# Attention on one core: value products of two key blocks together, at the later step

## What is computed

```python
# per batch b: n = 512 tokens, 8 heads, query/key width 64, value width 16
x = layernorm(x)
q, k = split(x @ W_qk); v = x @ W_v
dots = einsum('bhid,bhjd->bhij', q, k) * SCALE
attn = softmax(dots + bias[None], axis=-1)
out  = einsum('bhij,bhjd->bhid', attn, v)
out  = out.reshape(b, n, 128) @ W_out + b_out
```

## Time and profile before

| | us |
|---|---|
| median of 3 runs (lowest, highest) | 1367.31 (1366.61, 1368.74) |
| the profiled execution | 1359.86 |
| its span, first to last instruction | 1358.1 |
| TensorE busy in the span | 1087.7 (80%) |
| VectorE busy | 957.2 (70%) |
| ScalarE busy | 898.7 (66%) |
| GpSimd busy | 513.2 (38%) |

### The profile page before, as it was taken

The page is one execution under the profiler, slowest core; times in us unless marked ns, Lnnn a source line. Parts: engine busy times, 40 slices in busy tenths (PEclk is TensorE's granted clock), DMA queues, the critical chain, the costliest instruction groups (busy, mean ns, idle before and its releaser), DMA issues. The chain is left out here.

```text
span 1358.1 us, 26011 instructions
## 1 busy us (share of the span) xinstructions
PE 1087.7 (80%) x7230; PEld 732.7 (54%) x7230; DVE 957.2 (70%) x2037; ACT 898.7 (66%) x1865; POOL 513.2 (38%) x318
## 2 busy tenths in 40 slices
PE   1776488878788787863895899999999999992697
PEld 1333366666666675651894345454454445541696
DVE  5899577778788788854664467685776768673465
ACT  1787698989889798941673466665766566660564
POOL 0467377677767767861443000101101010111244
PEclk9888699899899899977998799999999999995899
DMA  3000132223254235321332100000000000000321
GB/s 83 2 3 2 32 87 86 74 84 93 78 173 133 91 116 156 90 67 51 95 94 63 47 1 1 17 1 17 13 3 16 1 16 0 16 17 33 97 88 49
DMA packets 50616, 74.26 MB, mean 55 GB/s; under 512 B 7351, under 2 KB 28604, under 8 KB 50528
## 3 DMA queue, kind: packets, MB, share of 16 engines
q1 hardware_dynamic: 41504, 51.09, 13.2%
q0 software_dynamic: 5568, 12.66, 2.6%
q10 hardware_dynamic: 3456, 9.46, 2.3%
HBM read 57.86 MB, written 16.24 MB: 55 GB/s over the span
## 5 line engine op out<-in xcount | busy, mean ns | idle before, releaser
L951 DVE TENSOR_TENSOR_SCAN h<-d_a,p_dbu 128x1024 f32<-128x1024 f32 x128 | 291.0, 2282 | 79.3 <-ACT d_a L738 55.4
L685 POOL TENSOR_TENSOR h<-h,c_rep 128x1024 f32<-128x1024 f32 x128 | 301.5, 2366 | 113.9 <-DMA c_rep<-c_rows 71.1
L1833 ACT ACTIVATE at_probs<-at_scores,at_min 128x512 f32<-128x512 f32 x256 | 183.7, 722 | 136.0 <-DVE at_min L1943 87.0
L1195 POOL DMA_INDIRECT expert_rows<-r_row,r_dest x64 | 62.9, 982 | 503.7 <-DVEq L1121 488.2
L1943 DVE CUSTOM_DVE_ANT_0 at_scores<-at_p_scores,arena 128x512 f32<-128x512 f32 x256 | 174.4, 684 | 89.8 <-PE at_p_scores L1709 50.2
L828 PE MATMUL p_dbu<-ident,b_du_T 128*128 128x128 f32 x1024 | 189.6, 306 | 55.4 <-ACT b_du_T L731 52.9
L731 ACT ACTIVATE b_du_T<-arena,b_T 128x256 f32<-128x256 f32 (+1 forms) x512 | 216.9, 496 | 0.3 <-ACT arena L712 0.2
L828 PEld LDWEIGHTS p_dbu<-ident,b_du_T 128*128 128x128 f32 x1024 | 117.2, 150 | 119.9 <-issue 66.8
L738 ACT ACTIVATE d_a<-arena,a_exp 128x511 f32<-128x511 f32 (+1 forms) x256 | 169.3, 710 | 0.7 <-DVE h L951 0.6
L1716 PE MATMUL at_p_probs_T<-ident,at_probs 128*128 128x128 f32 x1024 | 158.9, 283 | 5.3 <-ACT at_probs L1833 4.6
L1716 PEld LDWEIGHTS at_p_probs_T<-ident,at_probs 128*128 128x128 f32 x1024 | 112.7, 142 | 91.2 <-issue 68.0
(11 more groups left out here) (211 smaller groups left out, 1484.1 us busy)
## 6 DMA issues: line engine op xcount, KB each, us to landing
c_rep<-c_rows SPq DMA_DIRECT2D x128, 256.0 KB, 3.3
f_row<-expert_rows SPq DMA_DIRECT2D x78, 129.0 KB
arena<-in_w_all ACTq DMA_DIRECT2D x8, 578.0 KB, 4.0
arena<-bias_by_distance ACTq DMA_DIRECT2D x8, 448.0 KB, 3.8
x_tok<-in_x SPq DMA_DIRECT2D x4, 512.0 KB, 5.4
x_tok<-x_between SPq DMA_DIRECT2D x8, 256.0 KB, 2.8
expert_rows<-f_pad SPq DMA_DIRECT2D x10, 129.0 KB, 3.1
expert_rows<-f_pad ACTq DMA_DIRECT2D x8, 129.0 KB, 3.1
```

The source lines that it names most:

```text
L685: nc.gpsimd.tensor_tensor(h[:, s % HS, :, :], h[:, s % HS, :, :], cc, ALU.mult).then_inc(prod_done, 1)
L951: nc.vector.tensor_tensor_scan(h[:, s % HS, :, :].rearrange("p c t -> p (c t)"), da[:, s % 2, :, :].rearrange("p c t -> p (c t)"), p_dbu[: ...
L1833: nc.scalar.activation(pr[:, s % 2, :], sc[:, s % 2, :], ACT.Exp, scale=-1.0, bias=mn[:, s % 2:s % 2 + 1]).then_inc(probs_ready, 1)
```

## The change

The key blocks 0 and 1 of a group, which were issued at two steps, are issued together at the second of them, and the key blocks 2 and 3 likewise. Six steps of a batch (10, 14, 18, 22, 26, 30) lose their 8 records, six (12, 16, 20, 23, 28, 31) have 16 in place of 8. Nothing else is changed.

```diff
--- before.py
+++ after.py
@@ -1719,8 +1719,8 @@
 
 
             VALUES_AT = {}
-            for v, at in enumerate(((10, 12, 14, 16), (18, 20, 22, 23), (26, 28, 30, 31))):
-                VALUES_AT.update({s: (v, j, j + 1) for j, s in enumerate(at)})
+            for v, at in enumerate(((12, 16), (20, 23), (28, 31))):
+                VALUES_AT.update({s: (v, 2 * j, 2 * j + 2) for j, s in enumerate(at)})
 
             def values(b, par, v, first, end):
```

## The result

The changed kernel takes 1373.45 us (median of 11 runs, 1370.32 to 1378.54), the kernel before 1366.61 us (median of 11 runs beside it, 1362.50 to 1370.01). The ratio is 1.0047, 95% interval 1.0032 to 1.0062: **slower by 0.47%, 6.4 us (4.4 to 8.5)**. The forecast was slower, by 3.4 us; the time lies in the range, the size was about half of what came. Measured again twice, the ratio was 1.0042 (1.0026 to 1.0058) and 1.0029 (1.0012 to 1.0047): 5.7 and 4.0 us. The mean of the three is 5.4 us.

What follows compares the result with a forecast made beforehand. Attention looked TensorE-bound, but waits between engines decide what a moved group brings. Six middle batches +2.28, jumps -0.26, first batch +0.18, last +1.18 gave +3.4 us on the median 1367.3: 1370.7 us, range 1366.0 to 1374.0.

Steps and rivals of the forecast that it cites:

- Steps 10 to 15: Middle batches: removals at steps 10 and 14 bring 0, the enlarged step 12 arrives in full at the logits; sum +0.43.
- the 0.43 of step 12: Step 12's group grows from 0.57 to 1.00 us, delaying its turn and, through a tight chain, the router's logits.
- Steps 16 to 0: Rest of a middle batch: additions of 0.43 against removals of up to 0.57, sum -0.05 us.
- step 18: Turn 19 must wait for exponential 19, so of the 0.57 removed only 0.19 us is gained.
- First and last batch: First batch, without router, +0.18 us; last batch, without projections or next scores as cover, +1.18 us.
- The jumps: Two loop jumps between batches: step 30's whole 0.57 comes through in place of 0.44, 2 x -0.13 = -0.26 us.
- Rival (c): The clock stays up at the two jumps: 3.4 - 1.2 = +2.2 us, 1369.5; chance 0.10.

Runs made afterwards that it cites:

- Filling the waits: Identity transposes added in TensorE's waits of steps 11 and 15: to the changed kernel (ratios to before 1.0018, 1.0003), to only the first group merged (1.0044, 1.0037).
- unfilled kernels: The changed kernel (ratios to before 1.0042, 1.0029) and the kernel before with only the first value group merged (1.0067), both without added transposes.

## Why the prediction was right in its sign and too small

**Steps 10 to 15: shown.** The removal at step 10 became wait (1.20 for 0.62), the 0.43 of step 12 arrived at the logits (6.95), and putting steps 10 and 12 back took it away.

**Steps 16 to 0: shown**, by the table of pairs. Only step 18 brought 0.13 where 0.19 was predicted: the handover to turn 19 (0.06) is as thought, but a turn that comes out of a wait is followed 0.49 later, not 0.44. The page TensorEngine Tiling (Array Packing) of the Trainium skill, in section Key Properties, has a drain at each change of tiling mode; the traces agree that a group has a price of its own (two groups of 8 records take 1.14, one of 16 takes 1.00), but show no drain as its cause; and by that rule alone the change would have been faster, and it is not.

**First and last batch: about right.** From the value projection in front of the first batch to the output product behind it the trace has 61.48 against 61.22: +0.26 (predicted +0.18). In the last batch the removals brought 0.08 at step 18 (2.57 against 2.65) and 0.44 at step 26 (2.21 against 2.65) where 0.19 and 0.57 were predicted, and steps 30 and 31 cost 0.31 (from the turns of step 28 to the last value group 4.51 against 4.20; predicted 0.36). That makes about +1.4, not +1.18.

**The jumps: right but for the clock.** Across the first jump a batch took 62.25 against 61.94, +0.31 with the clock down in both (predicted 0.38 - 0.13 = 0.25). Added up, four batches of 0.44, two of 0.31, 0.26 and 1.4 are **4.0 us**; the steps gave 3.4. Rival (c), that the clock stays up there because TensorE idles less, has no support: the second scores wait 1.41 in place of 1.84 at the first jump, and the clock fell at both jumps in two of the three profiles of the changed kernel, at none in the third, and at both in the two profiles of before. In all fourteen profiles it fell at 13 of the 16 jumps with the larger group at step 31 and at 10 of the 12 without it. Where it stays up more is won than the 0.6 I had allowed: 61.24 in place of 62.25 us.

**The term that was missing** is the step in which the removals of steps 10 and 14 were priced at 0. What they leave is wait, and I took wait to be free. Behind three waits in a row, 1.20, 0.31 and 0.75 us, TensorE's clock fell in two of three profiles of the changed kernel, at 1.57 us each, while behind the 0.62 and 0.57 of before it fell in neither profile. The sum of steps 4.0 and one fall of 1.57 are 5.6, against measured 6.4, 5.7 and 4.0, a mean of 5.4.

Open is the size of it. Filling the waits brought 3.7 us (give or take 2.2), more than the one fall that a profile shows, but by the granted clocks a part of that seems to be gained elsewhere. Against the kernel before, the unfilled kernels' executions have 5.7, 0.8 and 6.0 us more at the lower level by the same estimate (as above, in the order of the table), one or two falls, with an uncertainty as large. Fillers in the kernel before, which would part the two effects, weren't tried.

## What to carry to other kernels

Before work is moved in a hand-written order, mark for each step which wait ends last there. A group taken out of a step that ends in a wait on another engine brings nothing, and a group put in front of the operation that such a chain starts from is paid in full, though the moved work is the same and its overhead even shrinks. The first group's merges, placed into the waits (steps 10 and 15) instead of in front of the chain and behind it (steps 12 and 16), with the one merge left out that cost time (step 20), turned 0.4% slower into 1.1% faster.

## What the runs showed of the hardware that I had not expected

- TensorE's granted clock fell to its lower level after a row of short waits, none over 1.21 us. It had been busy for 2.94 of the 4 us ahead of the fall, against 3.43 in the kernel before at the same place and 3.37 with fillers (850.34 to 854.34). The fall came in four of the 35 batches with these waits in the five profiles, each time in the same place of a batch (steps 15 and 16). At the jumps, after a wait of 1.3 to 2.0 us (3.7 once), the clock fell in 23 of 28 cases.
- How long it stays down at a jump differs between executions of one kernel. In the profiles of the changed kernel, with and without fillers, a batch across a jump takes 61.1 to 61.4 us where the clock stays up, about 62.3 after a short fall (granted clock 0.83 over 944 to 954) and 63.8 to 64.0 after a longer one (0.74 over 1064 to 1077).
- Work without any use can pay: twelve transposes in a batch's waits made two kernels 3.7 us faster (the mean of three pairs, give or take 2.2), with each batch as long as without them in the traces that have no fall.
- The stretch ahead of attention, the same in all kernels, took between 747.6 and 768.5 us in the profiled executions, and the two ends are both of the kernel before, whose second profile I had expected at 750 to 757. That is three times the effect in question, so a single profile of each kernel must be compared by stretches, not by spans.
